# Host-side layout of weights and vectors, set-up split by layer, and scores issued in equal pairs, in a fused attention and feed-forward kernel

## The reference, cut to what matters

```python
# conditioning: cross attention, 16 heads of 16
q = (side + b_self) @ Wq + bq
k = concat([x + b_prev, side + b_self]) @ Wk + bk
v = concat([x, side]) @ Wv + bv          # each query sees all of x and its own token of side
y = softmax(q k / 4, masked by length) @ v @ Wo + bo
for l in range(2):                        # two layers
    q, k, v = split(shift(y) @ wqkv[l])   # 8 heads of 64
    q, k = rotary(l2norm(q) * q_scale, l2norm(k) * k_scale)
    y += local_attention(q, k, v) @ wo[l] # blocks of 128 queries; keys of own and previous block
    h = layernorm(shift(y)) * ln_g + ln_b
    a, g = split(h @ w1[l] + b1[l])       # 682 + 682 columns
    y += (a * gelu(g)) @ w2[l] + b2[l]
out = x + y
```

## Time and profile before

| | us |
|---|---|
| median of three runs | 3585.71 |
| lowest, highest | 3585.01, 3586.89 |
| the profiled execution's own time | 3581.24 |
| its span (first to last instruction) | 3579.4 |
| TensorE busy | 3496.0 |
| VectorE busy | 2571.0 |
| ScalarE busy | 2314.2 |

### The profile page before, as it was taken

The page is one execution under the profiler, slowest core; times in us unless marked ns, Lnnn a source line. Parts: engine busy times, 40 slices in busy tenths (PEclk is TensorE's granted clock), DMA queues, the critical chain, the costliest instruction groups (busy, mean ns, idle before and its releaser), DMA issues.

```text
span 3579.4 us, 58380 instructions
## 1 busy us (share of the span) xinstructions
PE 3496.0 (98%) x20454; PEld 2482.8 (69%) x20454; DVE 2571.0 (72%) x7124; ACT 2314.2 (65%) x5077; POOL 743.4 (21%) x883
## 2 busy tenths in 40 slices
PE   6799999999999999999999999999999999999997
PEld 3567777777777777777777777777777777777765
DVE  3577777777777777777777777777777777777764
ACT  1357667667667667667667667667667667667764
POOL 1122221122221222221222221212221212221211
PEclk6899999999999999999999999999999999999999
DMA  5111111011111011111011111111111111111000
GB/s 152 25 25 25 31 31 31 20 18 25 31 31 31 20 18 25 31 31 30 20 18 25 31 31 31 22 16 25 31 31 31 24 18 21 31 31 25 7 7 10
DMA packets 104721, 99.34 MB, mean 28 GB/s; under 512 B 15304, under 2 KB 103152, under 8 KB 104432
## 3 DMA queue, kind: packets, MB, share of 16 engines
q1 hardware_dynamic: 99104, 85.91, 14.5%
q10 hardware_dynamic: 5328, 9.70, 0.8%
HBM read 35.80 MB, written 8.39 MB: 12 GB/s over the span
## 4 chain that ended last, share of the span: by engine, by line
PE 94%; ACT 2%; DVE 2%; SPq 1%; issue 1%; DMA 1%; POOLq 0%; POOL 0%; DVEq 0%; ACTq 0%
PE ps L1127 15%; PE ps L1020 12%; PE ps L1138 8%; PE ps L1071 6%; PE ps L1103 6%; PE ps L1034 6%; PE ps L1093 5%; PE ps L1082 5%; PE ps L935 4%; PE ps L925 3%; PE ps L908 3%; PE ps L1054 3%; PE ps L879 3%; PE ps L889 3%; PE ps L960 2%; PE ps L1131 2%
## 5 line engine op out<-in xcount | busy, mean ns | idle before, releaser
L635 POOL TENSOR_TENSOR inv<-ssq_f,minus_half 128x16 f32<-128x16 f32 x128 | 419.3, 3276 | 1083.4 <-DVE ssq_f L1358 1083.4
L763 ACT ACTIVATE attn_area<-attn_area,f_nb,inv 128x128 f32<-128x128 f32 (+1 forms) x1024 | 546.6, 537 | 116.8 <-DVE f_nb L1386 116.0
L1127 PE MATMUL ps<-feed_area,w_s 128*128 128x256 f32 x2560 | 607.5, 383 | 4.2 <-DVE feed_area L1421 3.7
L1127 PEld LDWEIGHTS ps<-feed_area,w_s 128*128 128x128 f32 x2560 | 468.2, 191 | 82.7 <-issue 16.0
L1295 DVE TENSOR_REDUCE c_mx<-ps 128x2 f32<-128x512 f32 x512 | 348.9, 688 | 146.5 <-PE ps L908 144.2
L716 ACT ACTIVATE cond_area<-ps 128x512 f32<-128x512 f32 x512 | 299.2, 592 | 78.0 <-PE ps L925 73.9
L1382 DVE CUSTOM_DVE_ANT_0 attn_area<-ps,cst 128x128 f32<-128x128 f32 (+1 forms) x1024 | 303.4, 351 | 60.4 <-issue 59.2
L1432 DVE SCALAR_TENSOR_TENSOR feed_area<-ps,b_s,feed_area 128x256 f32<-128x256 f32 (+1 forms) x448 | 214.1, 478 | 126.7 <-ACT feed_area L789 112.8
L1138 PE MATMUL ps<-feed_area,w_s 128*128 128x256 f32 x1280 | 292.5, 380 | 0.3 <-DVE feed_area L1432 0.3
L1397 DVE TENSOR_SCALAR attn_area<-attn_area,f_inv 128x128 f32<-128x128 f32 (+1 forms) x1024 | 258.1, 316 | 9.1
L466 DVE COPY attn_area<-ps 128x384 f32<-128x384 f32 x256 | 142.1, 555 | 167.6 <-PE ps L1082 167.5
(11 more groups left out here) (158 smaller groups left out, 6575.4 us busy)
## 6 DMA issues: line engine op xcount, KB each, us to landing
cond_area<-cond_area SPq DMA_DIRECT2D x384, 128.0 KB, 4.6
res_rows<-in_x SPq DMA_DIRECT2D x32, 256.0 KB, 2.7
out<-res_rows SPq DMA_DIRECT2D x32, 256.0 KB, 2.1
x_rows<-in_x SPq DMA_DIRECT2D x31, 256.0 KB, 2.7
f_rows<-in_fside_BxSxS SPq DMA_DIRECT2D x31, 256.0 KB, 3.0
wqkv_s<-in_L_ffn_wqkv ACTq DMA_DIRECT2D x2, 1536.0 KB
w_s<-in_L_ffn_w ACTq DMA_DIRECT2D x2, 1364.0 KB
cond_area<-cond_area SPq DMA_DIRECT2D x128, 6.0 KB
```

The source lines that it names most:

```text
L635: nc.gpsimd.tensor_tensor(inv[:, l, t, :], ssq_f[:, l, t, :], minus_half[:, :], ALU.pow).then_inc(SL[l]["inv_norm"], 1)
L763: nc.scalar.activation(soft[:, h % SOFT, lo:hi], soft[:, h % SOFT, lo:hi], ACT.Exp, bias=f_nb[:, l, q, h:h + 1], scale=inv[:, l, q, h:h + ...
L1127: last = mm(ps[:, N0 + f % 2, c * N:(c + 1) * N], w1_s[:, l, k, lo:lo + P], hn[:, k, :], start=(k == 0), stop=(k == KD - 1))
```

## The change

Four things, of which the first three are the set-up.

1. **Layout on the host.** `Wq`, `Wk` and their biases come permuted; `w1` has its columns in the order gate, value, rest (1386 instead of 1364, so `w1_last` goes); `w2` comes padded; all vectors by channel are one array `columns` of 42 columns; the scales are one row.
2. **Loads in order of use.** SyncE issues ten loads, the rows of sequence 1, then the placing of sequence 0 and its maxima, and only then the weights of the layers, seven loads (`load_layers`). `w1` of layer 0 is the fifth load of ScalarE's queue. Each group has a semaphore of its own.
3. **Set-up by layer.** The 22 products of layer 0 (44 instructions) stand in front of TensorE's first score of sequence 0, those of layer 1 in front of the first `mean`; VectorE scales `w1` of layer 0 in front of `mix` 0 and that of layer 1 in front of its first `mean`. The strings of `HEAD` are new; `ORDER` and `TAIL` stay.
4. **Scores in equal pairs.** New order and new places in PSUM (`SCORE_PARTS`); `own_scored` goes, one wait (`third_scored`) remains.

```diff
+SCORE_PARTS = {(0, 0): (0, 0), (2, 0): (0, 1), (0, 1): (0, 2), (1, 1): (1, 0), (1, 0): (1, 2), (3, 0): (1, 3),
+               (2, 1): (2, 0), (3, 1): (2, 2)}
...
         def score_part(h, q):
-            i = h % 4
-            if q == 0:
-                at = ((i % 2) * 2 + i // 2) * P
-                return ps[:, t_bank("scores", 3 * (h // 4) + 2), at:at + P]
-            return ps[:, t_bank("scores", 3 * (h // 4) + i % 2), (i // 2) * N:(i // 2 + 1) * N]
+            bank, at = SCORE_PARTS[h % 4, q]
+            at *= P
+            return ps[:, t_bank("scores", 3 * (h // 4) + bank), at:at + (q + 1) * P]
...
+            load(ident, consts[:, C_IDENT:C_IDENT + P], ident_loaded)
+            tiled(cw_s[:, :, D:2 * D], wk, wk_loaded)
+            load(cols[:, :], columns, cols_loaded)
+            tiled(cw_s[:, :, 0:D], wq, wq_loaded)
+            load(brow, rows_b[0:1, 0:2 * D].broadcast_to([P, 2 * D]), bias_loaded)
+            load(cst[:, C_MASK:C_COS], consts[:, C_MASK:C_COS], bias_loaded)
...
+            def load_layers():
+                tiled(wqkv_s[:, 0], wqkv[0], qkv_loaded[0])
+                tiled(wo_s[:, 0], wo[0], back_loaded[0])
+                tiled(w2_s[:, 0], w2[0], back_loaded[0])
+                tiled(wqkv_s[:, 1], wqkv[1], qkv_loaded[1])
+                tiled(w1_s[:, 1], w1[1], w1_loaded[1])
...
-            sp.wait_ge(setup_pool, 15)
+            next_rows(0)
+            sp.wait_ge(setup_pool, 14)
             place_parts(0)
             load_maxima(0)
+            load_layers()
             load_residual(0)
...
+            load(cw_s[:, :, 2 * D:3 * D], wv, wv_loaded)
+            load(cwo_s[:, :, :], cwo, wv_loaded)
+            load(w1_s[:, 0], w1[0], w1_loaded[0])
...
+            def b1_products(l):
+                def products():
+                    pe.wait_ge(w1_loaded[l], 16)
+                    pe.wait_ge(setup_pool, 11)
                     for c in range(W1T):
                         m = P if c < W1T - 1 else LASTW
                         for k in range(KD):
...
+                            last = mm(ps[0:m, N0 + 1, l * W1T + c:l * W1T + c + 1], w1_s[:, l, k, c * P:c * P + m],
+                                      ln_bs[:, l, k:k + 1], start=(k == 0), stop=(k == KD - 1))
+                    last.then_inc(b1_product, 1)
+                return products
...
-                    for i, q in ((0, 0), (1, 1), (0, 1), (1, 0), (2, 1), (3, 0), (3, 1), (2, 0)):
+                    for i, q in ((2, 1), (1, 1), (0, 0), (1, 0), (2, 0), (3, 0), (0, 1), (3, 1)):
                         h = first + i
                         r, p, keys = FDH * (h % 2), h // 2, (q + 1) * P
-                        if (i, q) == (1, 0):
-                            pe.wait_ge(SL[l]["own_scored"], upto(seq, "own_scored", 2 * t + 1))
-                        elif (i, q) == (2, 0):
-                            pe.wait_ge(SL[l]["own_scored"], upto(seq, "own_scored", 2 * t + 2))
+                        if (i, q) == (3, 1):
+                            pe.wait_ge(SL[l]["third_scored"], upto(seq, "third_scored", t + 1))
...
+            setup = {(0, "project", 0): key_biases, (0, "part", 1): row_biases, (0, "project", 3): wv_there,
+                     (0, "score", 0): b1_products(0), (0, "mean", (0, 0)): b1_products(1),
+                     (0, "variance", (0, 0)): biases_read}
+            for l in range(DEPTH):
+                setup[0, "qk", (l, 0, 0)] = setup[0, "value_rows", (l, 0)] = qkv_there(l)
+                setup[0, "out_proj", (l, 0)] = back_there(l)
+                setup[0, "hidden", (l, 0)] = scaled(l)
...
+            run(dve, "DVE", step, {(0, "part", 1): key_side, (0, "project", 1): masks, (0, "project", 3): values_there,
+                                   (0, "score", 0): rotation_tables, (0, "rotate", (0, 0)): turns_made,
+                                   (0, "mix", 0): norm_weights(0), (0, "mean", (0, 0)): norm_weights(1)})
```

More of the change, by code:

```diff
@@ L60 @@
 C_COLS = C_SIN + TILES * 2 * FDH
+V_PREV = 0
+V_SELF = V_PREV + KD
+V_BK = V_SELF + KD
+V_BO = V_BK + KD
+V_B1 = V_BO + KD
+V_B2 = V_B1 + DEPTH * W1T
+V_G = V_B2 + DEPTH * KD
+V_B = V_G + DEPTH * KD
+V_COLS = V_B + DEPTH * KD
+W1C = 2 * HFULL * P + LASTW
 ACT_TURNS = (1, 3, 5, 7)
@@ L480, in _, with load, tiled @@
         def _(sp):
-            def load(dst, src, loaded, column=False):
-                sp.dma_start(dst, src, allow_slow_non_contiguous=column).then_inc(loaded, 16)
-            def row(v, width):
-                return v.rearrange("(a n) -> a n", a=1).broadcast_to([P, width])
+            def load(dst, src, loaded):
+                sp.dma_start(dst, src).then_inc(loaded, 16)
+            def tiled(dst, src, loaded):
+                load(dst, src.rearrange("(k p) n -> p k n", p=P), loaded)
             def load_rows(seq):
@@ L516, in _ @@
-            for l in range(DEPTH):
-                load_vectors(l)
-            for s, scales in enumerate((q_scale, k_scale)):
-                load(qk_sc[:, :, s, :], scales.rearrange("(a l) d -> a l d", a=1).broadcast_to([P, DEPTH, FDH]), layers_loaded)
-            load(turns, consts[:, C_COS:C_COLS], layers_loaded)
+            load(ident, consts[:, C_IDENT:C_IDENT + P], ident_loaded)
+            tiled(cw_s[:, :, D:2 * D], wk, wk_loaded)
+            load(cols[:, :], columns, cols_loaded)
@@ L855, in cond @@
                         pe.wait_ge(S["x_start"], upto(seq, "x_start", 0))
-                    pe.wait_ge(S["rows_loaded"], upto(seq, "rows_loaded", 32))
-                    for s, rows in enumerate((x_rows, f_rows)):
+                    for s, (rows, loaded) in enumerate(((x_rows, "rows_loaded"), (f_rows, "side_loaded"))):
+                        pe.wait_ge(S[loaded], upto(seq, loaded, 16))
                         for k in range(KD):
@@ L1490 @@
     arrays, args = {}, []
[L1491 to L1492 removed]
+    for name, a in laid_out(inputs).items():
+        a = np.ascontiguousarray(a)
         arrays[f"in_{name}"] = a
```

397 lines of the change are left out of this document (177 added, 220 removed).

## The result

The changed kernel takes 3533.3 us (median of 4 runs, 3531.7 to 3534.6) against 3585.4 of the kernel before (median of 4, 3582.1 to 3586.9): a ratio of 0.9856, 95% interval 0.9839 to 0.9873. It is 52 us faster. The prediction said 69 us and 3517; the result lies in its range, 16 us above its value. The profiled execution took 3532.6 us with a span of 3530.7 (3579.4 before), so the spans differ by 48.7 us. I first show where these come from, and then where the missing ones went.

A forecast was written before the change was run, and what follows sets the result against it. TensorE's stream of columns was taken to bound some 3200 us, latency the first 183 us. Scores 38, the gap at 87 us 19 and the front 12 made 69 us: 3585.7 - 69 = 3517 us, range 3500 to 3540.

The forecast's parts named there:

- Part 1: Score matmuls in equal pairs: each of 128 groups takes 1.50 us instead of 1.84, worth 38 us at the end.
- I take off a tenth: Score groups: deduction from 42 us to 38 for chains begun ahead of a group and awaited behind it.
- my lower bound of 24: Score groups: the gain if 128-column matmuls go at 0.14 us instead of 0.11 and a quarter is lost to waits.
- Rival (a): Steady passes: new waits of 0.2 to 0.3 us behind each score group leave 10 us there, time 3545; chance 0.13.
- My reason for 1.50 us: Score groups: 0.34 us go from each, put down to unequal pairs and the two waits on `own_scored`.
- the 34.1 us of "issue": Idle time ahead of score weight loads, 34.1 of 64.8 us, taken as the visible part of the two waits.
- Part 2: Gap at 87 us: 20.9 us of set-up leave it and come back in two halves by layer; 19 us won.
- The term that I had mis-sized: Conditioning of sequence 1, up to its last matmuls at 181.40: taken as 67.4 us in the new stretch of 70.5.
- Part 3: The front: first score at about 31.5 us saves 8.5, faster first maxima save 3.5; together 12 us.
- (b): Score groups: weight loads not hidden behind matmuls of their own half, 2.27 us per group, time 3610; chance 0.02.
- (c): Dense stretch: gaps gather and the clock falls; with 7 us per sequence the time is 3625; chance 0.03.
- Rival (d): Set-up gives half, since a late load or longer products take its place: 3533; chance 0.14.

## Why the prediction was right or wrong

**Part 1: the group right, its worth at the end wrong.** 1.50 us forecast, 1.51 measured, 128 groups. The step that failed is "I take off a tenth". I had argued that VectorE and ScalarE "start their part when the scores are there, so they mostly move along". Two of the four groups are followed by a step that awaits a chain which started ahead of the scores, and these lose all of their 0.33 us, not a tenth. Part 1 gave 20 to 22 us instead of 38, below my lower bound of 24. That bound was also added up wrong: slots of 0.14 us leave 0.22 us per group, 120 x 0.22 + 8 x 0.11 = 27 us, and less a quarter 20, not 24. That the result meets 20 is luck, for the slots stayed short and the waits took a half. The sentence behind it, "a chain that began ahead of a score group and is awaited behind it loses 0.34 us of cover", names the right mechanism; the step that I left out was to look, for each of the four groups, at what TensorE waits for next and where that chain began. The trace of before did hold the answer: 11.10 us from `weigh` to the transposes, with an `f_nb` of 0.93 us in it.

**Rival (a)** forecast 10 us for part 1, one wait behind each group. It was half right: two groups, not four. Its sign came, idle time named ahead of the turns of probabilities (0.37 us at L1069). The truth lies in the middle between forecast and rival.

**My reason for 1.50 us** is shown in part although the number was met. I put the gain down to unequal pairs and to the two waits, without a share for either. By the traces 0.14 us stand at one of the two waits and nothing at the other, and an unequal order without such idle time takes 0.52 us more; the 0.19 us left are not divided by any run. One reading was wrong: the 34.1 us of "issue" are not the visible part of the waits. They stand ahead of the first load of a group, some 0.36 us in 94 of the 128, and are still 35.0 us in the changed kernel.

**Part 2**: 19 us forecast, 15 found. The forecast was for the stretch from the end of sequence 0's `Wo` to the first mean, 96.2 us before and 1.3 + 67.4 + 1.8 + 6.5 = 77.0 us after. Measured it is 81.2 us, from 71.85 to 153.03: 0.9 up to the rows of sequence 1, 72.3 of its conditioning, 1.7 of its last matmuls, 6.2 of products where 5.5 were put, and nothing for VectorE behind them. The term that I had mis-sized is the 67.4 us, taken as they stood from the trace of before. The two stretches, before and after:

```profile
114.04:181.40 67.36, 54.81 (x330) 33.02 (x329) 44.20 (x118) 32.32 (x78) 14.68 (x21) 0.90 0.23 33
72.78:145.08 72.30, 61.26 (x337) 36.08 (x338) 45.55 (x118) 33.07 (x79) 14.54 (x21) 0.81 0.25 48
```

TensorE is busy 6.5 us longer there, at a granted clock of 0.81 instead of 0.90. The set-up alone has 72.6 us, so the score groups are not the cause; why the clock was lower is not shown. Just ahead, the clock gave 2.3 us: from the first use of the maxima to the end of `Wo` it is 35.7 us before, at 0.50 throughout, and 33.4 us after, at 0.66. With the 12.9 us of the front, 12.9 + 2.3 + 15.0 = 30.2 us are won by the first mean.

**Part 3**: 12 us forecast. The first score won 9.4 us (8.5 said), the maxima 3.4 (3.5 said), 12.9 together. Both causes were confirmed by putting them back. By the Trainium skill's rule on issue time, cited with the experiment, part 3 would have been 6.

**Parts 2 and 3 together**: 31 us forecast, 30.5 measured alone. In part this is luck: what the conditioning of sequence 1 cost more, part 3 and the clock ahead of it gave back.

**Rivals (b) and (c)** did not come. No weight load stood in the way: a group of 1.51 us, where (b) says 2.27; the Trainium skill's rule on row groups, on which it rested ("TensorE: Matmul & The Clock Gate", section "The mechanism" of part 3), is not borne out here. The clock stayed at 1.00 in the dense stretch, with 0.6 us of each pass lost again. **Rival (d)**, at 3533, hit the time for the wrong reason: the set-up gave all of its gain.

The sum, mended: 31 + 21 = 52 us.

## What to carry to other kernels

Before an operation on the busiest engine is shortened, follow for each of its places the next wait behind it to where that chain begins: if it begins ahead of the operation and does not go through it, the gain is worth only the slack that the wait has today, and a chain that takes equally long in both traces is the sign. Look in such a chain for a tiny operation with a long duration, and at what another engine does in that moment; moving that one operation here gave some 15 us more, and it costs a line. A wait for one's own result should stand as many instructions behind it as the order allows. And a length that is taken over from a trace carries the granted clock of its stretch with it: 67.4 us became 72.3.

## What the runs showed of the hardware

- VectorE's `f_nb` (two inputs from SBUF, 128 x 4) took 1.23 us instead of 0.16 while GpSimd made a 128 x 512 product, and ended within 0.03 us of it. With the product elsewhere it took 0.17. I had not looked for this. The Trainium skill ("GPSIMD Engine Reference", section "1. Specifications") says that GpSimd shares its access to SBUF with VectorE, with contention where a VectorE instruction has two inputs from SBUF; this trace agrees.
- A semaphore wait on TensorE for a matmul issued directly ahead cost 0.54 us in a group of 1.51, with 0.25 us of idle time ahead of the weight load. For a matmul two places ahead this idle time was 0.14 us, for three places 0.03; with seven places the group took what the sum without waits gives.
- DMAs of 128 x 5 single elements held SyncE's queue 12.66 us for eight, from 0.43 to 6.86 us each. Two weight loads of 1536 and 512 KB held ScalarE's own queue 2.2 and 3.7 us; its next copy came 3.2 us later than in the changed kernel.
- Instructions of one column took 0.21 us each at a granted clock of 0.50 and 0.14 us at 0.75.
